# Matrix products of the main stage issued in pairs of 64 stationary columns

## The reference

```
x = x + attention0(layernorm(x), ctx)     # 16 heads of 64, keys and values from ctx
x = x + ffn0(layernorm(x))                # silu(x Wg) * (x Wu), then Wd; 768 hidden
x = x + attention1(layernorm(x), ctx)     # as attention0 with other weights
x = x + quantised(layernorm(x))           # rows to 8 bits, one 256 x 256 product, scaled back
```

## Time and profile before

| | us |
|---|---|
| median of three runs | 1677.54 |
| the profiled execution | 1680.52 |
| its span | 1678.7 |
| TensorE products, busy | 1600.9 (95%) |
| loads of stationary operands, busy | 1308.8 (78%) |
| VectorE, busy | 1367.8 (81%) |
| ScalarE, busy | 1381.0 (82%) |
| GpSimd, busy | 1267.2 (75%) |

### The profile page before, as it was taken

One profiled execution on the slowest core, in us unless ns is written; L12 is line 12 of the kernel. 1 busy time (PEld: TensorE's weight loads), 2 busy tenths in 40 slices (PEclk: granted clock), 3 DMA queues, 4 the chain that ended last, 5 costly groups with the idle time before them and its releaser, 6 DMA issues.

```text
span 1678.7 us, 52618 instructions
## 1 busy us (share of the span) xinstructions
PE 1600.9 (95%) x16048; PEld 1308.8 (78%) x16048; DVE 1367.8 (81%) x3505; ACT 1381.0 (82%) x5650; POOL 1267.2 (75%) x1888
## 2 busy tenths in 40 slices
PE   6999866999999999999999999999999999999995
PEld 3555545788888888888888888878888888888884
DVE  5666655888888888888888887788888888888885
ACT  4555556889889889899899888888999999999994
POOL 3000146898898898898898887788888888888884
PEclk9999988999999999999999999999999999999998
DMA  8777859899878889788888998889999999999995
GB/s 207 229 243 238 264 131 195 157 167 181 171 163 178 173 165 178 169 168 175 176 164 177 174 163 159 163 150 193 194 187 192 195 187 188 196 191 187 187 191 106
DMA packets 874333, 305.34 MB, mean 182 GB/s; under 512 B 752529, under 2 KB 862001, under 8 KB 874225
## 3 DMA queue, kind: packets, MB, share of 16 engines
q1 hardware_dynamic: 872960, 299.39, 86.7%
q0 software_dynamic: 1264, 4.72, 0.9%
HBM read 87.72 MB, written 65.54 MB: 91 GB/s over the span
## 4 chain that ended last, share of the span: by engine, by line
PE 40%; POOL 32%; issue 12%; DMA 1%; DVE 1%; POOLq 0%; SPq 0%; ACT 0%; ACTq 0%
PE psum L998 11%; PE psum L985 11%; POOL pr L1476 10%; POOL p L1483 8%; PE psum L974 7%; PE psum L1013 6%; POOL p L1479 6%; POOL hT_l L1466 3%; POOL rs L1455 2%; PE psum L1022 2%; PE psum L960 1%; PE psum L1029 1%; POOL y L1504 1%; PE psum L1035 1%; POOL x_res L1492 1%
## 5 line engine op out<-in xcount | busy, mean ns | idle before, releaser
L1159 ACT ACTIVATE ex<-psum,nmax 128x77 f32<-128x77 f32 x2048 | 639.0, 335 | 49.2 <-DVE nmax L1321 44.9
L1159 ACT ACTIVATION_READ_ACCUMULATOR ex<-psum,nmax 128x1 f32 x2048 | 440.7, 215 | 0.0
L1483 POOL TENSOR_TENSOR p<-pr,p 128x308 f16<-128x308 f32 x512 | 406.0, 793 | 38.5
L1476 POOL TENSOR_TENSOR pr<-ex,rden 128x308 f32<-128x308 f32 x512 | 381.5, 745 | 64.4 <-DVE rden L1326 63.8
L985 PE MATMUL psum<-xT,wq_h 128*128 128x256 f16 x2048 | 353.5, 275 | 1.4 <-DVE xT L1240 1.4
L1321 DVE TENSOR_REDUCE nmax<-psum 128x4 f32<-128x308 f32 x512 | 242.0, 473 | 83.5 <-PE psum L974 77.5
L998 PE MATMUL psum<-wo_h,oT_h 128*128 128x256 f16 x1024 | 280.5, 274 | 22.7 <-DVE oT_l L1240 22.7
L985 PE MATMUL psum<-xT,wq_l 128*128 128x256 f16 x1024 | 281.2, 275 | 0.0
L998 PE MATMUL psum<-wo_l,oT_h 128*128 128x256 f16 x1024 | 279.9, 273 | 0.0
L998 PE MATMUL psum<-wo_h,oT_l 128*128 128x256 f16 x1024 | 279.8, 273 | 0.0
L974 PE MATMUL psum<-kb,qT_h 128*128 128x154 f16 x2048 | 257.8, 231 | 8.3 <-DVE qT_l L1243 3.9
(11 more groups left out here) (157 smaller groups left out, 3302.0 us busy)
## 6 DMA issues: line engine op xcount, KB each, us to landing
keys<-ks SPq DMA_DIRECT2D x14, 1408.0 KB, 6.3
kb<-keys SPq DMA_DIRECT2D x256, 77.0 KB, 3.6
vb<-vals SPq DMA_DIRECT2D x128, 154.0 KB
vals<-vs SPq DMA_DIRECT2D x56, 256.0 KB, 2.3
x_pair<-in_x_dram SPq DMA_DIRECT2D x32, 256.0 KB, 3.1
pT<-p SPq DMA_TRANSPOSE x512, 3.4
x_res<-in_x_dram SPq DMA_DIRECT2D x32, 256.0 KB, 3.4
mid_x<-y SPq DMA_DIRECT2D x32, 256.0 KB, 2.4
```

The lines of the kernel that those rows point to most:

```text
L1159: last = act.activation(ex[i][:, t, b, :], SC[:, t, b * NK:(b + 1) * NK], ACT.Exp, bias=nmax[i][:, t, b:b + 1], accum_out=den[i][:, t, b:b ...
L1476: pool.tensor_tensor(pr[:, t, :, :], ex[i][:, t, :, :], r, ALU.mult).then_inc(s_p, 1)
L1483: pool.tensor_tensor(d[:, t, 1, :, 0:NK], pr[:, t, :, :], d[:, t, 0, :, 0:NK], ALU.subtract).then_inc(s_pl, 1)
```

## The change

A helper `halves` takes the place of the single product in `scores`, `queries`, `project`, `gate_up`, `down` and `quantised`. It issues two products in a row with the same moving operand and the same flags: stationary columns 0 to 63 into PSUM partitions 0 to 63, columns 64 to 127 into partitions 64 to 127. `weigh_values`, the transposes and the whole first stage stay as they are. The semaphore is raised by the second product of the last pair.

```diff
--- before.py
+++ after.py
@@ -961,6 +961,12 @@
                                                 (ident if src.dtype == F32 else ident16)[:, :])
                     return last
 
+                def halves(o, w, x, **flags):
+
+                    for b in range(2):
+                        last = pe.matmul(o[b * DH:(b + 1) * DH], w[:, b * DH:(b + 1) * DH], x, **flags)
+                    return last
+
                 def scores(k, u, t, k_need):
                     if t == 0:
                         pe.wait_ge(s_ql, k + 1)
@@ -971,7 +977,7 @@
                         o = SC[:, t, a * 2 * NK:(a + 1) * 2 * NK]
                         ts = slice(t * P, (t + 1) * P)
                         for q, (w, part) in enumerate(((qT_h[i], 0), (qT_h[i], 1), (qT_l[i], 0))):
-                            last = pe.matmul(o, w[:, a, ts], kb[u // 2][:, part, u % 2 * PPU + a, :], start=(q == 0),
+                            last = halves(o, w[:, a, ts], kb[u // 2][:, part, u % 2 * PPU + a, :], start=(q == 0),
                                              stop=(q == 2))
                     last.then_inc(s_s, 1)
 
@@ -982,7 +988,7 @@
                         terms = [(ww, part, k) for k in range(KT) for ww, part in
                                  ((wq_h[l], 0), (wq_h[l], 1), (wq_l[l], 0))]
                         for q, (ww, part, k) in enumerate(terms):
-                            last = pe.matmul(oo, ww[:, k, w], xT[par][:, :, part, k, :], start=(q == 0),
+                            last = halves(oo, ww[:, k, w], xT[par][:, :, part, k, :], start=(q == 0),
                                              stop=(q == len(terms) - 1))
                     last.then_inc(s_q, 1)
 
@@ -995,7 +1001,7 @@
                             for q, (oo, ww) in enumerate(((oT_h[u % 2], wo_h[l]), (oT_l[u % 2], wo_h[l]),
                                                           (oT_h[u % 2], wo_l[l]))):
                                 first = u == 0 and t == 0 and a == 0 and q == 0
-                                last = pe.matmul(OA[:, t, :], oo[:, a, ts], ww[:, m, :], start=first,
+                                last = halves(OA[:, t, :], oo[:, a, ts], ww[:, m, :], start=first,
                                                  stop=(u == UNITS - 1 and a == PPU - 1 and q == 2),
                                                  skip_group_check=True)
                     if u == UNITS - 1:
@@ -1019,20 +1025,20 @@
                         oo = o[:, a, :].rearrange("p (t q) -> p t q", q=P)
                         terms = [(k, part) for k in range(KT) for part in range(2)]
                         for q, (k, part) in enumerate(terms):
-                            last = pe.matmul(oo, w[:, k, c * P:(c + 1) * P], x2T[:, :, part, k, :], start=(q == 0),
+                            last = halves(oo, w[:, k, c * P:(c + 1) * P], x2T[:, :, part, k, :], start=(q == 0),
                                              stop=(q == len(terms) - 1))
                     last.then_inc(s_g, 1)
 
                 def down(t, o):
                     terms = [(c, hh) for c in range(HC) for hh in (hT_h, hT_l)]
                     for q, (c, hh) in enumerate(terms):
-                        last = pe.matmul(o[:, 0, :], hh[:, c, t * P:(t + 1) * P], wdT[:, c, :], start=(q == 0),
+                        last = halves(o[:, 0, :], hh[:, c, t * P:(t + 1) * P], wdT[:, c, :], start=(q == 0),
                                          stop=(q == len(terms) - 1))
                     last.then_inc(s_d, 1)
 
                 def quantised(t, o):
                     for k in range(KT):
-                        last = pe.matmul(o[:, 0, :], qiT[:, k, t * P:(t + 1) * P], rhs_q[:, k, :], start=(k == 0),
+                        last = halves(o[:, 0, :], qiT[:, k, t * P:(t + 1) * P], rhs_q[:, k, :], start=(k == 0),
                                          stop=(k == KT - 1))
                     last.then_inc(s_a1, 1)
```

## The result

The changed kernel takes 1741.01 us (median of four runs, 1734.02 to 1745.65), the kernel before 1677.65 beside it: a ratio of 1.0372 [1.0335, 1.0409]. It is 3.7% slower, well outside the range. The profiled execution took 1745.65 us with a span of 1743.9, 65.2 more than the 1678.7 before.

A forecast was written before the change was run, and what follows sets the result against it. TensorE was taken to set the pace, losing time at value-group borders. 26 us saved, less 24 for eleven refetching turns and 1 for shared DMA, gave a gain of 1 us: 1676.5 from 1677.5, range 1650 to 1698.

The forecast's parts named there:

- The borders: Around each value group, 64-column products next to 128-column ones lose 0.22 us at two borders; pairs remove both, 0.90 us a batch.
- What is kept of it: Of 0.90 us a batch, 0.72 stays in layer 0 and 0.12 in layer 1; together 26 us saved.
- three new borders: At layer 1's two transpose groups, which stay whole: three new borders at 0.11, 0.33 us a batch lost.
- The pairs cost nothing: On TensorE a pair costs no more than one product: 0.109 us for 256 moving columns, 0.067 for 154.
- the forecast's estimate: By the skill's formula, two 64-column loads in a row for each score pair would cost 124 us more; not taken.
- The hand-out of instructions: TensorE's sequencer must hand out instructions twice as fast, one every 27 ns, in scores every 17; taken as costing nothing.
- Whether the code is held: Layer 0 loop body, some 2000 instructions, is fetched anew at each turn; layer 1 body, 1480, is held.
- The price of a turn: Each layer 0 loop turn costs 2.2 us (0.35 to 2.85) for fetching code, eleven turns 24 us.
- rival 3: Layer 0 turn's fetch above 2.4 us makes it slower; two blocks in a row: 1689 to 1701 us; chance 0.17.
- the sharing of DMA engines: Code fetches share DMA engines with keys and values; 88 packets more on engines with 16% to spare, 1 us added.

The follow-up runs named there:

- Straight pairs: All pairs as in the changed kernel, but TensorE's program is straight code in all rounds, no hardware loop: 1706.7 us, 1.0156 against the kernel before.
- 1492: Against the kernel before: pairs in three of eight layer 0 loop stretches, all straight main-stage rounds and layer 1, with VectorE's output sum moved later there: 1670.31 us, 0.9953.
- 1564: Kernel before with pairs only in the odd rounds of the layer 0 loop, single products everywhere else: 1782.64 us, 1.0611.
- 1763: Layer 1 body when the kernel before, all single products, has TensorE loops of four batches a turn (layer 0 body 2258 instructions): 1751.26 us, 1.0425.
- the short pause: Kernel before with useless semaphore increments at the end of TensorE's loop bodies, 30 in layer 0 and 14 in layer 1: 1757.9 us (one run).
- the pairs of layer 0 alone: Kernel before with pairs up to round 33 only, layer 0 as straight TensorE code, layer 1 single products in its loop: 1685.95 us, 1.0040.
- straight single products: Kernel before, single products, with TensorE's program as straight code in all rounds: 1684.04 us, 1.0035.

## Why the prediction was wrong, point by point

**The borders: right.** Behind the projection the value group starts after 0.11 us instead of 0.20, and what follows it starts 0.10 us earlier as well. From the last projection product to the first scores it is 0.77 us instead of 0.98, so 0.21 a group, where I had taken 0.22.

**What is kept of it: too much in both layers.** In layer 0 the wait behind `oT_l` came as said (0.17 for 0.15), but a second one of 0.24 at `down` was missed. Kept are 0.42 us a batch, not 0.72. I had followed one chain, the one with the smallest slack, and not asked for the next. In layer 1 I forecast a gain of 0.12 us a batch and got a loss of 0.14. The three new borders cost 0.25 us at the first transposes (the last rows of this text) and 0.10 at the second, 0.35 for a forecast of 0.33. But only seven of the eight old ones are gone: the one from the transposes to the values stays, 0.33 us from the first of them to the first value product, 0.32 in the earlier trace rows, and I had counted it as gone. The waits for `oT_l` take more than what is left.

**The pairs cost nothing: right**, 0.109 and 0.066 us a pair. The loads of a pair are 0.11 us long each, yet pairs of 256 columns stay at the pace of one product. The Trainium skill (TensorE: Matmul & The Clock Gate, Weight-path perf modes) has a fast path for loads of the full 128 columns only; what its loss would have cost by the forecast's estimate, 124 us, was not seen.

**The hand-out of instructions: right only for held code.** Straight pairs in layer 1 had 19.0 us of waits for "issue" from 1267 to 1560 us.

**Whether the code is held: right for both loops, with a poor reason.** Layer 0 (1996 instructions) is not held, layer 1 (1476) is. I had the 2048 of the Trainium skill (Runtime: NRT & Kernel Launch, Instruction fetch mechanics) in mind. Here 1492 was held, 1564 was not, and 1763 only sometimes. The measurement decides, and the room that these bodies had was smaller.

**The price of a turn: the step that failed.** Forecast were 2.2 us; the borders' gain apart, the turn lost 6.9. By the rows, for one turn (the 1.9 us are half of the time at half clock in which products ran, 20.9 us over eleven turns, and the short pause gave the same):

| | us |
|---|---|
| hole behind the branch (32.7 / 10, and 0.16 that the length of a record hides) | 3.4 |
| products at half clock behind it | 1.9 |
| `x2T` late (9.4 / 10) | 0.9 |
| `hf` late (2.0 / 10), and `oT_l` once 0.16 | 0.4 |
| eight groups at 0.21 | -1.7 |
| sum | 4.9 |
| measured, 55.46 - 50.23 | 5.2 |

The hole is 1.2 us longer than forecast, mostly as the branch takes 4.1 us where I had 3.15. I priced the fetch by data transfers of 2.3 and 3.6 us, and gave as a reason that they wait for the same queue; by the table of queues code comes on q8 and data on q1. The longer hole alone would have been inside rival 3, at 1690. The half clock behind the hole was in no case of mine, though it costs 11 x 1.9 = 21 us; I had seen only stretches without pauses and taken the clock as given. And I had put the sharing of DMA engines at 1 us in all, by their spare share, where what counts is one transfer: `x2T` had 0.2 to 0.8 us of slack, and a code packet of about 1 us in front of it uses that up. That is another 10 us. Added up for the layer 0 loop: forecast were 7.9 us more than before (24 batches at -0.72, eleven turns at 2.2, and 1), measured 59.7. The longer holes are 13 of the difference, the half clock 21, `x2T` 9 beyond the 1, and what the pairs kept too little 7 (24 x 0.30): 50 of 52. Rival 3 had the right sign and place, and half the price.

**What is not settled.** Whether it is a limit by size alone is open: from 1492 (held) to 1564 (not held) the place of the body in the code changed too, and why 1763 was held at two jumps of five was not tried. Nor was what makes the second hole. How long a pause must be for the clock to fall can't be read from these runs. In the rounds of the two loops pauses of up to 1.6 us never did it, all of 2.7 us and more did, and between them it went both ways: three of 1.70 to 1.76 in straight pairs and one of 1.65 in the changed kernel were followed by half clock, one of 1.86 and one of 2.15 in the pairs of layer 0 alone were not. The 2 us in the expectation for the short pause was a guess. That code packets delay `x2T` is shown by the straight single products, but by how much a single one does was not measured.

## What to carry to other kernels

Before a loop body on TensorE grows, count its instructions: while it was held here (to 1492), jumping back cost 0.2 us and nothing else, and not held it cost 5.4 us a jump (1996, the pairs' gain included) to 10.5 (2258, with a second hole). Price a stall on TensorE as the stall plus the slow products behind it; here 3.5 us of pause cost 5.5. And spend a change that costs code only where the code has room and the chain behind it has slack: three eighths of this one in the layer 0 loop, with the sum moved in layer 1, made the kernel 0.5% faster, while all of it made it 3.7% slower.

## What the runs showed of the hardware that I had not expected

- A jump to code that is not held makes one hole or two, and the size of the body does not tell which: two with 1564 and 2258 instructions, one with 1996. With 1564 there are 72.4 us of waits in ten turns, with 1996 only 32.7.
- TensorE at 2.4 GHz went to 1.2 GHz behind all pauses of 2.7 us and more, whether a fetch or 30 idle increments (3.5 us) filled them, and stayed at 2.4 GHz behind 1.2 to 1.3 us. Behind 1.65 to 1.76 us it went to 1.2 GHz in four places, while behind 1.86 and 2.15 us it stayed in two.
- Packets of 16 KB of code on the DMA engines, 0.9 to 2.0 us long in the trace, make a transposing DMA land later: after at most 3.5 us with none in the loop, up to 4.9 with 46 (straight single products), and 4.2 in the median with 90 (changed kernel).
- The borders at transposes cost as much as those at value groups or a little more. Four transposes in layer 1, scores ahead of them and a projection behind (products, changed kernel):

```profile
1311.92 0.23 PE L967 MATMUL psum<-kb,qT_l 128*64 128x154 f16 x2
1312.08 0.66 PE L960 MATMUL psum<-ident,x_pair 128*128 128x128 f32 x4
1312.67 0.30 PE L967 MATMUL psum<-wo_h,oT_h 128*64 128x256 f16 x2
```

  From 1311.92 to 1312.67 it is 0.75 us; with single products, from 1306.25 to 1306.75, 0.50.
